# TTT scan of a two-layer decoder: latent slots, running sum and gradient stores placed elsewhere

## The reference

```
x = _layernorm(x + _L0_attn_ref(x, ...))      # test-time training (TTT), the sublayer that changes
x = _layernorm(x + _L0_xattn_ref(x, ctx, ctx))
x = _layernorm(x + _L0_ffn_ref(x, ...))
x = _layernorm(x + _L1_attn_ref(x, ...))
x = _layernorm(x + _L1_xattn_ref(x, ctx, ...)) # latent attention: weights w_kc_q, W_qr, W_kr, Wo, ...
x = _layernorm(x + _L1_ffn_ref(x, ...))        # mixture of experts
```

```
def step(carry, x):
    W1_s, b1_s = carry
    xq, xk, xv, eta_mb = x
    Z1 = xk @ W1_s + b1_s
    grad = _ln_fused_l2_bwd(Z1, xv - xk, ln_w, ln_b)
    Attn1 = jnp.tril(xq @ xk.swapaxes(-1, -2))
    b1_bar = b1_s - jnp.tril(eta_mb) @ grad
    Z1_bar = xq @ W1_s - eta_mb * Attn1 @ grad + b1_bar
    last_eta = eta_mb[:, :, -1, :, None]
    W1_new = W1_s - (last_eta * xk).swapaxes(-1, -2) @ grad
    b1_new = b1_s - jnp.sum(last_eta * grad, axis=-2, keepdims=True)
    out = xq + _ln(Z1_bar, ln_w, ln_b)
    return ((W1_new, b1_new), out)
```

## Time and profile before

| | us |
|---|---|
| median of 3 runs | 1221.96 (1221.21 to 1223.48) |
| the profiled execution's own time | 1214.36 |
| its span, from the first to the last instruction | 1212.5 |
| TTT: first block, scan, third block begins | 0 to 40.2, 40.2 to 191.6, 191.6 |
| busy in the span: PE, PEld, DVE, ACT, POOL | 88%, 54%, 70%, 48%, 22% |

### The profile page before, as it was taken

The page is one execution under the profiler, slowest core; times in us unless marked ns, Lnnn a source line. Parts: engine busy times, 40 slices in busy tenths (PEclk is TensorE's granted clock), DMA queues, the critical chain, the costliest instruction groups (busy, mean ns, idle before and its releaser), DMA issues. The chain is left out here.

```text
span 1212.5 us, 24138 instructions
## 1 busy us (share of the span) xinstructions
PE 1067.6 (88%) x8866; PEld 659.5 (54%) x8866; DVE 847.3 (70%) x1996; ACT 587.6 (48%) x1596; POOL 271.4 (22%) x341
## 2 busy tenths in 40 slices
PE   9798686999979998798998978689999998789955
PEld 5366554777633333245555447477777775344422
DVE  3598864999858888479985897734477878733325
ACT  2356433454346667463552427167777775222212
POOL 5311100111111111305333110400000001157842
PEclk9788757999989999999999989999999999889987
DMA  6723331000013322070000002085000100669556
GB/s 197 114 82 113 95 123 59 2 2 2 2 53 102 113 78 79 10 144 1 1 1 1 2 1 76 15 272 161 19 18 19 31 19 24 189 186 246 86 130 260
DMA packets 83104, 94.81 MB, mean 78 GB/s; under 512 B 19808, under 2 KB 66918, under 8 KB 82726
## 3 DMA queue, kind: packets, MB, share of 16 engines
q1 hardware_dynamic: 73676, 79.79, 22.5%
q0 software_dynamic: 6368, 9.50, 4.2%
q10 hardware_dynamic: 2944, 3.98, 0.9%
HBM read 68.65 MB, written 21.97 MB: 75 GB/s over the span
## 5 line engine op out<-in xcount | busy, mean ns | idle before, releaser
L401 DVE TENSOR_REDUCE gqa_x_slots<-gqa_scores 128x8 f32<-128x1024 f32 x64 | 78.4, 1226 | 27.8 <-PE gqa_scores L288 18.8
L1571 DVE TENSOR_REDUCE mla_neg_max<-mla_scores 128x8 f32<-128x1024 f32 x32 | 39.2, 1224 | 77.2 <-PE mla_scores L1436 51.6
L1518 ACT ACTIVATE mla_probs<-mla_scores,mla_neg_max 128x128 f32<-128x128 f32 x256 | 90.1, 388 | 0.0
L358 ACT ACTIVATE gqa_expT<-gqa_scoresT 128x1024 f32<-128x1024 f32 x64 | 65.5, 1024 | 46.6 <-PE gqa_scoresT L309 46.6
L309 PE MATMUL gqa_scoresT<-gqa_x_slotsT,gqa_keys 32*128 32x512 f32 x256 | 72.6, 639 | 8.9 <-issue 4.8
L288 PE MATMUL gqa_scores<-gqa_keys_bd,xT 32*128 32x512 f32 x256 | 72.6, 663 | 2.7 <-DVE gqa_x_slots L401 1.4
L1426 PE MATMUL mla_q_ps<-xT,mla_merged_home 128*128 128x128 f32 x512 | 64.3, 280 | 1.9 <-PEq L63 1.9
L1426 PEld LDWEIGHTS mla_q_ps<-xT,mla_merged_home 128*128 128x128 f32 x512 | 61.3, 197 | 2.3 <-issue 2.1
L1459 PE MATMUL mla_out_ps<-mla_merged_home,mla_attT 128*128 128x256 f32 x256 | 60.7, 380 | 0.7 <-ACT mla_attT L1531 0.7
L1518 ACT ACTIVATION_READ_ACCUMULATOR mla_probs<-mla_scores,mla_neg_max 128x1 f32 x256 | 58.4, 228 | 0.0
L2645 PEld LDWEIGHTS ttt_z_ps<-ttt_g_pairs,ttt_masked 128*64 128x64 f32 x1024 | 51.5, 138 | 11.5 <-issue 10.7
(11 more groups left out here) (466 smaller groups left out, 2625.6 us busy)
## 6 DMA issues: line engine op xcount, KB each, us to landing
moe_w_gu<-in_moe_w_gu SPq DMA_DIRECT2D x24, 384.0 KB, 5.2
gqa_keys_bd<-in_gqa_keys_bd SPq DMA_DIRECT2D x16, 512.0 KB, 3.3
moe_w_dn<-in_moe_w_down SPq DMA_DIRECT2D x24, 192.0 KB, 6.6
moe_sums<-moe_zeros SPq DMA_DIRECT2D x2, 2176.0 KB, 11.9
ttt_by_token<-ttt_g_pairs SPq DMA_DIRECT2D x4, 576.0 KB, 5.1
ttt_lanes<-ttt_by_token SPq DMA_DIRECT2D x16, 144.0 KB, 5.5
xT<-in_x_feat SPq DMA_DIRECT2D x4, 512.0 KB, 7.9
x_tok<-in_mla_woT SPq DMA_DIRECT2D x8, 256.0 KB, 3.0
```

Source lines behind the costliest of these rows:

```text
L358: nc.scalar.activation(expT[:, k % 2, 2 * u:2 * u + 2, :], scoresT[:], ACT.Exp, scale=HD ** -0.5).then_inc(exp_ready, 1)
L401: nc.vector.tensor_reduce(x_slots[:, b % 2, :, c * NJ + 2 * half:c * NJ + 2 * half + 2, HD].rearrange("p g j -> p j g"), scores[:, of].rea ...
L1518: ins = nc.scalar.activation(probs[:, k % NB, e, i, :], scores[:, k % 2, e, i, :], ACT.Exp, bias=neg_max[:, k % 2, e, i:i + 1], accum_out= ...
```

## The change

- The latent slot of a half-step stands behind `outputs` and `turn_keys` on PE, and the fill ahead of `outputs` instead of behind `turn_keys`. ACT's copies of a latent slot come one half-step later, and its copy of a fill one half-step earlier than before.
- The matmul with the running sum is a function of its own (`bias`) and is issued right behind `update`.
- The running sum is kept by one `scalar_tensor_tensor` on DVE behind each of the first 14 gradients. ACT's `scale_last` (14) and POOL's `keep_sum` (14) are gone, and so is the buffer `g_last`.
- The gradient stores of chunks 0 to 6 are issued by POOL's queue (7 x 8 DMAs), and of the last chunk's half X = 0 four by SP and four by POOL. `split_bias` of the middle runs on POOL in one piece behind the stores of chunk 4.
- `store_bias(1)` on SP stands ahead of the last latent slot. The last latent store, the wait for it and the load of `x_tok` are in the third block, ahead of the stores of X = 1.
- The Sqrt table load stands ahead of ACT's last four key copies in the first block, and `lay_keys(1, 0)` at the head of the scan block.

```
     def sync(self, sp, to_keys, to_out, first, last):
...
-        if last == self.SLOTS:
-            self.store(sp, last - 1, to_keys, to_out)
-            sp.wait_ge(self.stored, self.stored_by(last - 1))
+    def finish(self, sp, to_keys, to_out):
+        self.store(sp, self.SLOTS - 1, to_keys, to_out)
+        sp.wait_ge(self.stored, self.stored_by(self.SLOTS - 1))
...
-        def store_gradients(sp, n, pairs, stored):
+        def store_gradients(sp, n, pairs, stored, groups=range(NG)):
...
# first block, ACT
+                    act.wait_ge(set_, 1)
+                    nc.scalar.activation(unused[:], eps[:], ACT.Sqrt)
                     for g in range(2, NG):
                         keep_keys(g)
-                    act.wait_ge(proj_copied, NG * DH)
-                    lay_keys(1, 0)
-                    act.wait_ge(set_, 1)
-                    nc.scalar.activation(unused[:], eps[:], ACT.Sqrt)
...
# scan, SP
-                    sp.wait_ge(pairs_zeroed, 1)
                     for n in range(NC - 1):
                         if n and 2 * n < latent.SLOTS:
                             latent.sync(sp, *merged, 2 * n, 2 * n + 1)
-                        if n:
-                            for X in range(2):
-                                sp.wait_ge(grads_ready[X], n)
-                            store_gradients(sp, n - 1, slice(0, 2), g_stored[(n - 1) % SLOTS_G])
+                        if n == NC - 2:
+                            store_bias(1)
                         if 2 * n + 1 < latent.SLOTS:
                             latent.sync(sp, *merged, 2 * n + 1, 2 * n + 2)
-                    sp.dma_start(keep["x_tok"][:], io["x"].rearrange("b t d -> t b d")).then_inc(x_loaded, 16)
-                    store_bias(1)
-                    for X in range(2):
-                        sp.wait_ge(grads_ready[X], NC - 1)
-                    store_gradients(sp, NC - 2, slice(0, 2), g_stored[(NC - 2) % SLOTS_G])
+                    sp.wait_ge(pairs_zeroed, 1)
...
-                    store_gradients(sp, NC - 1, slice(0, 1), last_stored[0])
+                    store_gradients(sp, NC - 1, slice(0, 1), last_stored[0], range(0, NG // 2))
...
# scan, POOL
                     for n in range(NC - 1):
                         for X in range(2):
-                            keep_sum(X, n)
-                            step = 2 * (n - MIDDLE) + X
-                            if step == 0:
-                                pool.wait_ge(fill_copied, fills_by(BIAS_AT[1]) + 1)
-                            if 0 <= step <= PARTS:
+                            pool.wait_ge(grads_ready[X], n + 1)
+                        store_gradients(pool, n, slice(0, 2), g_stored[n % SLOTS_G])
+                        if n == MIDDLE:
+                            pool.wait_ge(fill_copied, fills_by(BIAS_AT[1]) + 1)
+                            for step in range(PARTS + 1):
                                 split_bias(1, step, mid, mid, parts1)
                     pool.wait_ge(half_cast, 1)
+                    pool.wait_ge(grads_ready[0], NC)
+                    store_gradients(pool, NC - 1, slice(0, 1), last_by_pool, range(NG // 2, NG))
...
# scan, ACT
+                    lay_keys(1, 0)
...
                             deviation(X, n)
-                            if s >= 2 and fill_of(s - 2):
-                                keep_fill(s - 2)
-                            if s and m < NC:
-                                scale_last(was, m - 1)
                             if n:
                                 keep_rows(X, n)
+                            if 0 <= s - 2 < latent.SLOTS:
+                                latent.scalar(act, s - 2)
+                            if s and fill_of(s - 1):
+                                keep_fill(s - 1)
                             if n < NC - 1:
                                 need(act, z_ready[X], n)
                                 lay_keys(X, n + 1)
-                            if 0 <= s - 1 < latent.SLOTS:
-                                latent.scalar(act, s - 1)
...
# scan, PE
                             update(X, n)
-                            if s < latent.SLOTS:
-                                need(pe, fill_copied, fills_by(s))
-                                latent.tensor(pe, s)
+                            bias(X, n + 1)
+                            if fill_of(s):
+                                fill(s)
                             outputs(X, n + 1)
                             turn_keys(X, n + 1)
-                            if fill_of(s):
-                                fill(s)
+                            if s < latent.SLOTS:
+                                need(pe, fill_copied, fills_by(s + 1))
+                                latent.tensor(pe, s)
...
# scan, DVE, at the end of gradients(X, n)
                         tt(rows(g), rows(gx), wide(coef[:, X]), ALU.mult).then_inc(grads_ready[X], 1)
+                        if n < NC - 1:
+                            dve.wait_ge(grads_ready[X], n + 1)
+                            need(dve, sum_kept[X], n)
+                            dve.wait_ge(z_ready[X], n + 1)
+                            if n == MIDDLE:
+                                dve.wait_ge(fill_ready, fills_by(BIAS_AT[X]) + 1)
+                            total = g_sum[:, X].rearrange("p b e -> p (b e)")
+                            stt(total, g, neg_last[:], total, ALU.mult, ALU.add).then_inc(sum_kept[X], 1)
...
# third block, SP
+                latent.finish(sp, *merged)
+                sp.dma_start(keep["x_tok"][:], io["x"].rearrange("b t d -> t b d")).then_inc(x_loaded, 16)
                 store_gradients(sp, NC - 1, slice(1, 2), last_stored[1])
...
# third block, PE, apply(b): for b == 0
+                            pe.wait_ge(last_stored[0], 16 * NG // 2 * QQ)
+                            pe.wait_ge(last_by_pool, 16 * NG // 2 * QQ)
```

More of the change, by code:

```diff
@@ L2375, in turn_keys, with bias @@
                         ins.then_inc(rows_turned, 1)
-                    def outputs(X, n):
+                    def bias(X, n):
                         need(pe, z_copied[1 - X], n + X)
@@ L2380, in outputs @@
                         nc.tensor.matmul(z_ps1[:, X], same_lane[:], g_sum[:, X].rearrange("p b e -> p (b e)"), start=True, stop=False, skip_group_check=True)
+                    def outputs(X, n):
                         if n == 0:
@@ L2405, in fill @@
                         kind, m = fill_of(s)
-                        pe.wait_ge(latent.copied, s + 1)
+                        need(pe, latent.copied, min(s, latent.SLOTS))
                         if kind == "query":
@@ L2415, in _ @@
                     for X in range(2):
+                        bias(X, 0)
                         outputs(X, 0)
```

24 lines of the change are left out of this document (7 added, 17 removed).

## The result

The changed kernel takes 1215.04 us (median of 20 runs, 1207.44 to 1224.63), the kernel before 1219.80 on the same chip (20 runs, 1212.43 to 1225.80): ratio 0.9959, 95% interval 0.9940 to 0.9977. It is faster by 0.4%, 4.8 us; the forecast was 14.7 us. The profiled execution took 1211.38 with a span of 1209.6, 2.9 less than the 1212.5 of the kernel before, so the two traces can say where the forecast gain was lost.

What follows compares the result with a forecast made beforehand. DVE was taken to bound the scan at PE's high clock, PE at the low one. Drain -8.9, start -1.5, sum and port 0, scan's waits -4.3 gave -14.7 us: 1221.96 to 1207.3, range 1199 to 1217.

Steps and rivals of the forecast that it cites:

- What bounds the scan: TTT scan: DVE bounds it while PE's clock is high (2.4 GHz), PE while it is low (1.2 GHz).
- those without lose the clock now too: Scan: half-steps without queries (8, 10, 11, 12) already lose PE's high clock in the kernel before.
- The drain: From gradient 14 to the third block: 15.33 us falls to 6.35, -8.9 us, upper bound 9.3.
- The start: End of first block: table load and last lay_keys leave it; -1.5 us, bounds -2.5 and -1.2.
- Sum and port: Scan: DVE's added sum, +6.4 us, offsets POOL additions that held DVE, at most -6.7; about 0, bounds -0.5 and +3.
- POOL's issues: Scan: POOL's 60 DMA issues cost DVE 0; upper bound +32 us at 0.54 each.
- Rival (c): Scan: each of 60 POOL issues holds DVE; at the full 0.54 us the kernel takes 1239.7; chance 0.07.
- The other concern: POOL's queue: an issue waits for up to one DVE operation, 0.96 us each; the sum would not move.
- The scan's waits: Scan by half-steps: 117 us from gradient 0 to 14 against 121.24; -4.3 us, bounds -10.2 and +2.8.
- a half of the late part at either level: Late half-steps: half at PE's high clock, half at its low one, giving 117 us for the scan.
- (b): Late scan: low clock from half-step 7, latent loads and work set the pace; scan +2.8, 1214.4 us; chance 0.17.
- (a): Late scan: PE keeps the high clock; scan -10.2, in all -20.6, 1201.4 us; chance 0.20.

Runs made afterwards that it cites:

- e2_only_order: Kernel before with only the new order on TensorE and ScalarE, sum still on POOL, stores on SP; ratio 1.0109 to the kernel before.
- f3_both: Changed kernel with old TensorE/ScalarE order, an extra query in half-steps 8, 10, 11, 12, all last stores on SP; 1200.81 us, 0.9832 to the kernel before.
- g3_old_order_moved_queries: Changed kernel with old TensorE/ScalarE order, last stores on SP, queries moved from half-steps 1, 3, 5, 13 to 8, 10, 11, 12; 1202.09 us.

## Why the prediction was wrong

**What bounds the scan**: right. Two regimes, DVE at the high clock, PE at the low one. But "those without lose the clock now too" holds for half-steps 11 and 12 of the kernel before (0.58 and 0.50 granted) and not for 8 and 10 (0.92 and 1.00).

**The drain**, -8.9: measured -7.1. SP and POOL were done in time as worked out; what failed is "about 0.3 for the blocks' change". The change comes 5.24 us behind POOL's last issue when POOL has issued 60 DMAs. With the last four on SP the end is 6.36, forecast 6.35. Nothing came back in the third block: `x_tok` was issued at 191.81 and landed 9.7 us later, its first sum is at 213.76.

**The start**, -1.5: measured -5.1. Two things were missed. The first is the memset on POOL. The chain "now at 49.42 behind it" did not wait for it: its row says that it waited for ACT. And the memset does not hold DVE's operations beside it:

```profile
40.78 6.93 POOL L2269 MEMSET ttt_g_pairs<- 128x8192 f32 x1 [1.05 <-DMA ttt_by_token<-ttt_g_pairs]
```

```profile
46.31 0.42 DVE L2450 TENSOR_TENSOR ttt_xg<-ttt_xg,ttt_lanes 128x256 f32<-128x256 f32 x1
```

I had taken the rule of the earlier trace rows for every operation on POOL. The second is the clock: PE's passes from the first outputs on ran at the high clock. The way from them to DVE's chain became 2.7 us shorter, and no term of mine had that.

**Sum and port**, 0: right. The undisturbed half-step is 7.60, forecast 7.56, against 7.53 to 7.55 in e2_only_order, where POOL still adds. The splits still hold DVE: at 131.69 a two-input operation takes 0.79 instead of 0.42, beside POOL's cast of 0.61 that began at 131.60.

**POOL's issues**, 0 for DVE: right, 0.50 us each. Rival (c) is refuted. The other concern came from the Trainium skill ("DMA: Bandwidth & Descriptors", "SWDGE vs HWDGE vs iDMA"); by that section DVE locks GpSimd out of the SBUF state that holds the descriptors during 2-port perf mode, a condition that I had left out. The eight issues above take 4.07 us with DVE busy beside them, so none of these waited for a DVE operation.

**The scan's waits**, -4.3: this is the step that failed. It measured +10.2 (+7.0 with the order alone, +5.8 to +10.2 over five profiles), outside my bound of +2.8. The way was wrong and not only the size: the latent slot behind the outputs stands in front of the next update. Half-steps 0 to 7 took 56.0 against 52.9, 7 to 11 39.6 against 38 at the low clock, 11 to 14 35.9 against 33. Three assumptions in it were wrong. I took "a half of the late part at either level", but nearly all of it is at the low one: 0.56 granted over 7 to 14, against 0.68 before. I let the loads set the round, while at the low clock most of it is PE's own work, 10.2 us in half-step 8. And I priced the query in front of the outputs at 1 to 2 us between half-steps 11 and 14; at the low clock it takes 3.55. The gain I had seen, 5.4 us at half-step 11, is real, though SP's stores were not its cause: without them, in the old order, that half-step is still 13.8. I did not ask what the same move does to the half-steps beside it, where the slot used to lie between update and outputs while DVE was busy with the model's mask.

**Rivals.** (b), the latent round at the low clock, named the bound that took over. Its 1214.4 us is near the 1215.04 measured by luck: it had +2.8 for the scan where +10.2 came, -1.5 for the start where -5.1 came, -8.9 for the drain where -7.1 came, and it started from a median 2.2 us too high. (a) needed a high clock in the late half-steps, which only the kernels with added or moved passes had.

**Versions that beat both**: f3_both (1200.81 us) and g3_old_order_moved_queries (1202.09), ratios 0.9832 and 0.9831. They keep start, drain, DVE's sum and POOL's stores, drop the new order, and move the last stores to SP. g3_old_order_moved_queries does so without extra work. Their intervals overlap, so neither is shown to be the faster.

## What to carry to other kernels

Before moving work on an engine whose clock changes, price the move at both clocks and in every iteration, not only in the one whose wait it removes: work moved off one critical edge lands on another. It is worth trying whether wide passes in a place with slack pay for themselves through the clock; here they did, by 10.5 us of scan. And where POOL has issued many DMAs in a block, give the last ones to another queue.

## What the runs showed of the hardware that I had not expected

- A block whose last issues were POOL's ended later the more DMAs POOL had issued in it: 5.24, 5.08, 4.59 us behind its last issue for 60, 58 and 52 of them.
- A memset of 6.93 us on POOL left DVE's two-input operations at 0.42 us, while additions and a 4.87 us multiplication on POOL held them.
- From 110 to 125 us PE was busy 14.46 of 15 us at a granted 0.50 in the changed kernel, and 13.01 at 1.00 in the one with passes added to six half-steps.
- The same third block took 148.1 to 155.2 us by its granted clock, 0.99 to 0.93, from one profile to the next, which is more than the whole change gave.
